# Query and key dots of a linear attention in two column tiles of 32, alternating

## The reference, cut to what matters

```python
q = sigmoid(q); k = sigmoid(k)
k_sum = k.sum(axis=2); q_sum = q.sum(axis=2)
sink_incoming   = 1.0 / (((q + EPS) * (k_sum + EPS)[:, :, None, :]).sum(-1) + EPS)
source_outgoing = 1.0 / (((k + EPS) * (q_sum + EPS)[:, :, None, :]).sum(-1) + EPS)
conserved_sink   = ((q + EPS) * ((k * source_outgoing[..., None]).sum(2) + EPS)[:, :, None, :]).sum(-1) + EPS
conserved_source = ((k + EPS) * ((q * sink_incoming[..., None]).sum(2) + EPS)[:, :, None, :]).sum(-1) + EPS
```

## Time and profile before

| what | us |
|---|---|
| median of 3 runs | 1695.84 (1695.72 to 1699.32) |
| span of the profiled execution | 1690.6 |
| median less span: what lies around it | 5.2 |
| TensorE busy | 1555.0 |
| VectorE busy | 989.6 |
| ScalarE busy | 445.7 |
| GpSimd busy | 305.1 |
| the first set of dots in the chain that ended last | 16.82 |

### The profile page before, as it was taken

The page is one execution under the profiler, slowest core; times in us unless marked ns, Lnnn a source line. Parts: engine busy times, 40 slices in busy tenths (PEclk is TensorE's granted clock), DMA queues, the critical chain, the costliest instruction groups (busy, mean ns, idle before and its releaser), DMA issues.

```text
span 1690.6 us, 23793 instructions
## 1 busy us (share of the span) xinstructions
PE 1555.0 (92%) x8983; PEld 1214.2 (72%) x8983; DVE 989.6 (59%) x1767; ACT 445.7 (26%) x854; POOL 305.1 (18%) x191
## 2 busy tenths in 40 slices
PE   4798988897999999999998999998999999898998
PEld 3686877776777777877786788877757755676765
DVE  7878767889954672397256666665154511763332
ACT  4423111223311220130124242434215101441222
POOL 1000002053111031004001222212211000004565
PEclk9899998999999999999998999999999999899999
DMA  5122324341230020011001010100101322529343
GB/s 158 45 71 91 105 88 164 118 146 52 88 114 27 1 69 25 1 50 68 25 1 51 25 50 26 50 25 26 51 14 53 115 86 80 206 71 316 55 80 44
DMA packets 52138, 123.93 MB, mean 73 GB/s; under 512 B 8417, under 2 KB 28792, under 8 KB 44894
## 3 DMA queue, kind: packets, MB, share of 16 engines
q1 hardware_dynamic: 14026, 65.34, 11.3%
q10 hardware_dynamic: 28147, 46.81, 8.0%
q0 software_dynamic: 9856, 10.28, 3.5%
HBM read 92.87 MB, written 40.22 MB: 79 GB/s over the span
## 4 chain that ended last, share of the span: by engine, by line
PE 75%; DVE 11%; DMA 5%; issue 3%; ACT 3%; POOL 1%; PEld 0%; DVEq 0%; ACTq 0%; PEldq 0%; SPq 0%; POOLq 0%
PE ps L620 9%; PE ps L621 9%; PE ps L622 9%; PE ps L2288 6%; PE ps L678 4%; PE ps L680 4%; PE ps L631 4%; PE ps L632 4%; PE ps L633 4%; PE ps L939 3%; PE ps L3045 3%; PE ps L3067 3%; PE ps L826 2%; DMA d_w<-arena 2%; DMA arena<-d_w 2%
## 5 line engine op out<-in xcount | busy, mean ns | idle before, releaser
L620 PE MATMUL ps<-wslot,XH 128*125 128x512 f32 (+2 forms) x560 | 214.9, 384 | 5.4 <-DVE XL L1456 3.9
L621 PE MATMUL ps<-wslot,XH 128*125 128x512 f32 (+2 forms) x560 | 212.9, 380 | 0.0
L622 PE MATMUL ps<-wslot,XL 128*125 128x512 f32 (+2 forms) x560 | 212.6, 380 | 0.0
L2936 POOL CAST wslot<-arena 128x2048 fp32r<-128x2048 f32 x25 | 47.7, 1908 | 798.3 <-PEq L3013 428.5
L631 PE MATMUL ps<-XH,wslot 128*128 128x500 f32 (+1 forms) x336 | 123.2, 367 | 17.6 <-DVE XL L1456 10.6
L1461 DVE TENSOR_TENSOR arena<-ps,arena 125x512 f32<-125x512 f32 x150 | 98.2, 684 | 51.3 <-PE ps L622 45.3
L620 PEld LDWEIGHTS ps<-wslot,XH 128*125 128x125 f32 x560 | 104.8, 187 | 31.3 <-issue 4.4
L678 PE MATMUL ps<-CTr,Hhi 125*128 125x500 f32 (+1 forms) x360 | 125.0, 361 | 0.0
L632 PE MATMUL ps<-XH,wslot 128*128 128x500 f32 (+1 forms) x336 | 121.8, 362 | 0.0
L633 PE MATMUL ps<-XL,wslot 128*128 128x500 f32 (+1 forms) x336 | 120.9, 360 | 0.0
L622 PEld LDWEIGHTS ps<-wslot,XL 128*125 128x125 f32 x560 | 104.6, 187 | 22.7
(11 more groups left out here) (445 smaller groups left out, 3074.7 us busy)
## 6 DMA issues: line engine op xcount, KB each, us to landing
arena<-in_units SPq DMA_DIRECT2D x29, 1024.0 KB, 4.8
arena<-in_units SPq DMA_DIRECT2D x8, 2048.0 KB, 11.8
d_w<-arena ACTq DMA_DIRECT2D x10, 625.0 KB
d_wt<-arena ACTq DMA_DIRECT2D x10, 625.0 KB, 4.1
rows<-in_rows ACTq DMA_DIRECT2D x22, 256.0 KB, 4.0
d_kv<-V SPq DMA_DIRECT2D x20, 250.0 KB
arena<-d_kv SPq DMA_DIRECT2D x20, 250.0 KB
arena<-d_wt ACTq DMA_DIRECT2D x2, 2441.4 KB
```

Of the source, the lines that this page charges most:

```text
L620: pe.matmul(o, lhsT=xh[:, k, s], rhs=H4[:, k, 0:nw], start=k == 0, stop=False, skip_group_check=True)
L621: pe.matmul(o, lhsT=xh[:, k, s], rhs=L4[:, k, 0:nw], start=False, stop=False, skip_group_check=True)
L622: last = pe.matmul(o, lhsT=xl[:, k, s], rhs=H4[:, k, 0:nw], start=False, stop=k == K - 1, skip_group_check=True)
```

## The change

The output of the dots and shifts is cut into quarters of 32 partitions. Products with `blkQ` write partitions 0 to 31, products with `blkK` partitions 32 to 63, so each is a column tile of its own, with 32 columns of weights in place of 40. The loop is turned round: for each feature chunk the queries' product, then the keys'; each operand has its own start and stop. `blkK` holds its heads in columns 0 to 7. Number, size and moving operands of the products stay, and so does what is read from PSUM.

```diff
+            def quarter(o, blk):
+                return o[32:64] if blk is blkK else o[0:32]
+
             def shift_job(i, blks):
-                o = begin(("shift", i))[0:40, 0:2]
-                for blk in blks:
-                    for c in range(KC):
-                        last = pe.matmul(o, lhsT=blk[:, c, :], rhs=epsc.to_broadcast([128, 2]),
-                                         start=(blk is blks[0] and c == 0), stop=(blk is blks[-1] and c == KC - 1),
-                                         skip_group_check=True)
+                o = begin(("shift", i))[:, 0:2]
+                for c in range(KC):
+                    for blk in blks:
+                        last = pe.matmul(quarter(o, blk), lhsT=blk[:, c, 0:32], rhs=epsc.to_broadcast([128, 2]),
+                                         start=c == 0, stop=c == KC - 1, skip_group_check=True)
                 last.then_inc(mx_full, 1)
 
             def dot_job(name, i, pairs):
                 c0, w = CH[i]
-                o = begin(name)[0:40, 0:w]
-                for p, (blk, xT) in enumerate(pairs):
-                    for c in range(KC):
-                        last = pe.matmul(o, lhsT=blk[:, c, :], rhs=xT[:, c, c0:c0 + w], start=(p == 0 and c == 0),
-                                         stop=(p == len(pairs) - 1 and c == KC - 1), skip_group_check=True)
+                o = begin(name)[:, 0:w]
+                for c in range(KC):
+                    for blk, xT in pairs:
+                        last = pe.matmul(quarter(o, blk), lhsT=blk[:, c, 0:32], rhs=xT[:, c, c0:c0 + w], start=c == 0,
+                                         stop=c == KC - 1, skip_group_check=True)
                 last.then_inc(mx_full, 1)
...
-            head_block(2, acc12, blkK, 32)
+            head_block(2, acc12, blkK, 0)
...
-            head_block(3, acc12, blkK, 32)
+            head_block(3, acc12, blkK, 0)
```

## The result

The changed kernel takes 1684.7 us (median of 4 runs, 1682.26 to 1686.91), the kernel before 1697.58 us (4 runs, 1695.72 to 1699.64). The ratio is 0.9927, with a 95% interval of 0.9908 to 0.9946: 0.73% or 12.4 us less by that ratio, where 0.47% was forecast. Direction and overlap were right, the forecast gain was too small.

A forecast was written before the change was run, and what follows sets the result against it. TensorE was taken to bound the kernel, busy for 92% of the span. Terms of 8.0 + 0 + 0 - 0 = 8.0 us cut the span to 1682.6 us; with 5.2 us around it, 1687.8 us, range 1685.5 to 1696.5 us.

The forecast's parts named there:

- What bounds the stretch: From 1217 to 1300 us TensorE alone bounds; its only wait is 0.3 us of issue in front of a shift.
- Step (a): First set of dots: two column tiles stream at once, 8.8 us in place of 16.8, a gain of 8.0 us.
- Both rivals against overlap: First set of dots: half an overlap, 12.6 us, total 1691.6 (chance 0.14); no overlap, 16.8 us, total 1695.8 (chance 0.15).
- The estimate from the Trainium skill: First set of dots: 16.8/1.59 = 10.6 us, a gain of 6.2 us and a time of 1689.6 us.
- Step (b): All dots and shifts: 32 weight columns for 40 gain nothing, loads being hidden; second and third sets stay as before.
- the slower rival: All three sets of dots: 96 weight loads come into the open, 11.1 us more, 1707.0 us without overlap; chance 0.07.
- Step (c): First shift, 16 instructions in 0.70 us: between 0.35 and 0.7 us afterwards; gain counted zero, 0.35 us put into the range.
- Step (d): Entering and leaving the tiles: zero more, at most another 0.2 us at each of five exits, 1.0 us.
- Step (f): Behind the first set: slack of the first subtraction falls from 5.5 to 3.8 us, none used up; later work moves up.
- The sum: Whole kernel: 8.0 + 0 + 0 - 0 = 8.0 us gained, span 1690.6 to 1682.6 us, time 1687.8 us.
- The range: Whole kernel's time: 1685.5 to 1696.5 us, covering full overlap and no overlap, with about 0.08 left out.
- The base: Kernel before: median 1695.84 us, 5.2 us over the profiled span; the same 5.2 us was added to the new span.

The follow-up runs named there:

- tiles_in_turn: The changed kernel with the dots' loops turned back, all four query products and then all four key products: 1690.25 us, ratio 0.996 to the kernel before.
- the two further comparisons: The changed kernel measured twice more, unaltered, against the kernel before: 1688.65 us, ratio 0.9943, and 1686.35 us, ratio 0.994.

## Why the prediction was right or wrong

*What bounds the stretch* was right. TensorE's list of waits for 1219 to 1292 us in the changed kernel has again one entry, 0.3 us of issue ahead of a shift, and no wait for another engine came up. The wait on the reload of the arena is there again too, 1.2 us in place of 1.4.

*Step (a)* was right in kind and 0.4 us too careful: 8.5 us where 8.8 was said. What failed in it is the order within a chunk. It was said that the first half runs alone because halves are taken in order; in fact a key half passes the waiting query half, and pairs start 6 ns apart from the first one. Both rivals against overlap fell: the set is shorter by a factor of 16.89/8.50 = 1.99. The estimate from the Trainium skill, "TensorE: Matmul & The Clock Gate" (Part 3), 1.59 from its 2.38 for three tiles, was too low for this stream of 48 halves; four tiles gave 16.89/4.38 = 3.86. That row of the Trainium skill has 512 columns, so length is not the reason, and no run here has three tiles. The sentence of the Trainium skill on the same page that matmuls start in strict program order does not hold for tiles_in_turn, unless the order was changed on the way to the engine, which no trace shows.

*Step (b)* was right for the dots (the sink took 8.49 us in place of 8.50): the weight loads stay hidden, two in each 0.42 us, so the slower rival fell as well. From the first spread product to the last dot it was 39.92 us in place of 40.04, most of it in the second and third shift, 0.05 us each. The rule in the list of the same page of the Trainium skill, that a load overlaps running products only in another row group, does not hold here, where all loads use all 128 rows; its text also names loads into a background buffer, which no trace here tells apart.

*Step (c)* counted zero and had 0.35 us in the range: it was 0.36.

*Step (d)* was right: behind the first set the second value product starts 0.33 us after the first in both kernels (0.23 elsewhere), and nothing is added at the other exits either.

*Step (f)* put the slack of the first subtraction at 3.8 us. It ends at about 1233.3 (1232.63 and a share of the 1.59 us), TensorE comes at 1237.06: 3.8 us. The step that failed for the size is that everything behind the dots would simply move up, a change of the clock there being put at nothing without a reason. It held for every wait of this stretch, but not for the clock: the arrival 8.9 us earlier, measured from the first shift, took TensorE out of a 3.4 us stretch at half level, worth 1.55 us. No rival had this.

*The sum.* Shown by the traces: 8.39 (set) + 0.36 (shift) + 0.12 (source and sink, shifts included) + 1.55 (clock) = 10.4 us, where 8.0 stood. On 1697.58 us that is a ratio of 0.9939, inside all three intervals. The measured 12.4 us of the first comparison would then hold some 2 us of scatter on top, which the two further comparisons (9.7 and 10.2 us) do not show.

*The range.* Its lower end doesn't follow from its own terms: 8.4 + 0.35 us of gain and 1 us of scatter give 1695.84 - 9.75 = 1686.1 us, and 1685.5 was written. It matters little, since the 10.4 us shown already lead from 1695.84 to 1685.4; the way from there to 1684.7 is within the scatter.

*The base.* 1695.84 us was the median of three runs. The 5.2 us between it and the span were taken for what lies around an execution. In the changed kernel the profiled execution took 1685.05 us for a span of 1683.3: 1.75 us. Every other execution on record has 1.7 to 1.9 us between the two. With 1.75 us the profiled execution of before would have taken 1692.35 us, an estimate, 3.5 us less than the median. This cancels in the difference, but it was a sign of how far single executions scatter, and the 1 us allowed for that at the lower end was too little.

## What to carry to other kernels

Here float32 products with weights of 32 columns and 125 to 500 moving columns ran two or four at once in different quarters of the output partitions, almost to the full factor; one operand alone could be split by its moving columns (1.85 us in place of 3.46 for a source part). The first thing to try elsewhere is the same, with the tiles alternating at least every two float32 products. Then read what the shorter stage does to the vector chain behind it, and compare the granted clock behind the change, not only in it: a microsecond or two can come or go there by the moment of arrival alone.

## What the runs showed of the hardware

- Tiles are served out of order to a depth: with runs of 4, 6 and 8 halves for one tile, 0, 2 and 4 of them start without a partner, so that three waiting ones were passed each time. (Which tile a half belongs to is inferred from the pace of one tile.)
- The slots themselves do not grow: 0.42 us for 500 float32 columns with one or two tiles at work, and 96 halves of 250 or 125 columns in four tiles in 4.38 us.
- Short products overlap too: the 16 of the first shift, with 2 moving columns, take 0.27 us in two tiles with 32 columns of weights against 0.63 us in one with 40. The 8 of the second shift stay in one tile and take 0.24 us against 0.29, so most of it is the tiles and not the narrower weights.
- A stretch of 3.4 us at half clock behind a pause of 0.6 us appeared in seven of fourteen traces, always in the same ones by kernel; 1.67 us of extra work removed it, 3.35 us restored it, and it was worth 1.55 us.
